# The start of the last feed-forward moved into the attention's last turn, with the last batch's end spread over its first steps

## What is computed

```python
q, k = heads(src @ Wq + bq), heads(src @ Wk + bk)          # 8 heads of 16
attn = softmax(q @ k.T / 4)                                # per batch 8 x 512 x 512
out = sum over r of (attn * (adj == r)) @ heads(src @ Wv[r] + bv[r])
x = layer_norm(src + out @ Wo + bo, g1, beta1)             # the attention's end
ff = gelu(x @ W1 + b1) @ W2 + b2                           # 128 -> 512 -> 128
return layer_norm(x + ff, g2, beta2)
```

## Time and profile before

| | us |
|---|---|
| median of 3 executions | 1179.6 (1178.28 to 1179.81) |
| the profiled execution, its own time | 1180.0 |
| its span, first to last instruction | 1178.2 |
| TensorE busy / VectorE / ScalarE / GpSimd | 1074.4 / 933.2 / 735.2 / 613.2 |
| granted TensorE clock, mean | 0.968 |
| last turn with a batch, its first to its last matmul | about 990 to 1021.7 |
| end of batch 15 alone | 1021.7 to 1038.3 |
| feed-forward | 1036.6 to the end |

### The profile page before, as it was taken

One profiled execution on the slowest core, in us unless ns is written; L12 is line 12 of the kernel. 1 busy time (PEld: TensorE's weight loads), 2 busy tenths in 40 slices (PEclk: granted clock), 3 DMA queues, 4 the chain that ended last, 5 costly groups with the idle time before them and its releaser, 6 DMA issues. The chain is left out here.

```text
span 1178.2 us, 21859 instructions
## 1 busy us (share of the span) xinstructions
PE 1074.4 (91%) x6087; PEld 515.6 (44%) x6087; DVE 933.2 (79%) x2324; ACT 735.2 (62%) x1341; POOL 613.2 (52%) x513
## 2 busy tenths in 40 slices
PE   3699999999988699999999999999999999889996
PEld 3666766767656223333333333333333333234442
DVE  2888888888897678888888889888888888337777
ACT  3477787777875366656666666666665665544442
POOL 3322322322212088888888888788878877700000
PEclk7699999999999799999999999999999999879998
DMA  5321131221104123322332233313331320000000
GB/s 164 112 108 54 53 106 54 66 94 53 53 32 140 36 85 109 98 65 82 112 94 77 66 112 94 87 56 115 101 93 39 116 64 2 1 5 31 36 36 36
DMA packets 49547, 86.54 MB, mean 73 GB/s; under 512 B 8920, under 2 KB 35928, under 8 KB 44379
## 3 DMA queue, kind: packets, MB, share of 16 engines
q1 hardware_dynamic: 46586, 85.59, 23.6%
q10 hardware_dynamic: 2912, 0.40, 0.2%
HBM read 52.12 MB, written 29.36 MB: 69 GB/s over the span
## 5 line engine op out<-in xcount | busy, mean ns | idle before, releaser
L1491 DVE TENSOR_REDUCE top<-b_peak 128x1 f32<-128x512 f32 x488 | 320.4, 685 | 75.4 <-PE b_peak L1243 73.9
L1365 ACT ACTIVATE b_prob<-b_score 128x1024 f32<-128x1024 f32 x256 | 257.9, 1026 | 157.1 <-PE b_score L1258 112.2
L1628 POOL TENSOR_TENSOR b_picked<-b_prob,mask 128x512 f32<-128x512 f32 x192 | 233.7, 1237 | 62.2 <-ACT b_prob L1365 48.6
L1628 POOL TENSOR_TENSOR b_picked<-b_prob,b_mask 128x512 f32<-128x512 f32 x192 | 235.5, 1249 | 48.7 <-ACT b_prob L1365 38.2
L467 POOL TENSOR_SCALAR a_code<-a_adj_in 128x512 bf16<-128x512 int32 x64 | 73.6, 1150 | 93.6 <-DVE a_xw_n L896 66.1
L1062 POOL TENSOR_TENSOR a_hw_n<-a_hw,a_inv 128x512 f32<-128x512 f32 x16 | 23.3, 1456 | 176.1 <-DVE a_inv L889 169.0
L833 ACT ACTIVATE a_att<-a_att,a_least 128x512 f32<-128x512 f32 x128 | 91.8, 720 | 31.3 <-DVE a_least L862 31.3
L1243 PE MATMUL b_peak<-b_k_stack,b_q_stack 96*128 96x512 bf16 x256 | 98.4, 384 | 7.1 <-DVE top L1491 6.5
L1243 PE MATMUL b_peak<-shared 96*128 96x512 bf16 x232 | 90.4, 391 | 10.0 <-issue 6.1
L862 DVE CUSTOM_DVE_ANT_0 a_att<-a_att,a_no_edge 128x512 f32<-128x512 f32 x128 | 89.5, 716 | 2.6 <-issue 2.1
L1745 ACT ACTIVATE c_hid<-c_mid,bff 128x512 f32<-128x512 f32 x64 | 44.0, 688 | 62.9 <-PE c_mid L1723 62.9
(11 more groups left out here) (216 smaller groups left out, 2018.4 us busy)
## 6 DMA issues: line engine op xcount, KB each, us to landing
a_adj_in<-in_adj SPq DMA_DIRECT2D x16, 1024.0 KB, 5.3
scratch<-shared SPq DMA_DIRECT2D x32, 384.0 KB, 2.9
shared<-scratch SPq DMA_DIRECT2D x16, 768.0 KB, 6.2
scratch<-shared SPq DMA_DIRECT2D x32, 256.0 KB, 2.1
b_q_stack<-scratch SPq DMA_DIRECT2D x8, 768.0 KB, 5.4
b_k_stack<-scratch SPq DMA_DIRECT2D x8, 768.0 KB, 8.2
a_x_in<-in_x SPq DMA_DIRECT2D x16, 256.0 KB, 2.6
xs<-in_x SPq DMA_DIRECT2D x16, 256.0 KB, 5.6
```

Of the source, the lines that this page charges most:

```text
L1365: act.activation(prob[s % 2][:, 2 * u:2 * u + 2, :], score[u][:, :, :], ACT.Exp, scale=float(DH) ** -0.5).then_inc(sem("exp_ready"), 1)
L1491: dve.tensor_reduce(top[g][:, hh, c:c + 1], peak[hh % 2][:, :], AX.X, ALU.max, negate=True).then_inc(sem("peak_read"), 1)
L1628: pool.tensor_tensor(picked[(NR * s + rel) % 2][:, hh, :], prob[s % 2][:, hh, :], m, ALU.mult).then_inc(sem("picked_pool"), 1)
```

## The change

The function `feed_forward` becomes a class `FeedForward` with the same operations as methods, called from the attention's streams. Its buffers now lie in the memory `shared` that held the stacks of the even batches, `hid` in the first q stack's place, the others in the first k stack's. Its banks are those of `score` and `peak`, with `o_ps` for `back`.

Turn 16 is gone. In its place every engine has a `last()`, and after it straight code in which the feed-forward's steps 0 to 3 and the end of batch 15 alternate. Feed-forward step 0 on TensorE stands before the last `weigh_picked`. The pieces `o1`, `turn_o`, `out` and `y` of batch 15 stand between the products of steps 1 and 2; its statistics, inverse root and shift on VectorE stand between `add` and `norm` of batch 2, and its centring on ScalarE before step 4. The inverse root of batch 15 is taken on VectorE with the 11 tiny instructions in place of Ln and Exp on ScalarE. Batches 4 to 15 run as before, in a loop.

In steps 1 to 7 of the turn of batch 15, GpSimd makes two of the four picked heads and VectorE two (`FREE = 1`).

```diff
+        FREE = 1
...
+        ff = FeedForward(z, w, xs, out, shared,
+                         (score[0][:, 0, :], [score[0][:, 1, :], score[1][:, 0, :], score[1][:, 1, :], peak[0][:, :]],
+                          peak[1][:, :], o_ps[:, :]), sem("centred"), sb, lambda name: keep.enter_context(nc.semaphore("c_" + name)))
...
-            for b in range(B - 2, B + 1):
+            for b in range(B - 2, B):
                 turn(b, b % 2)
+            last()
...
+        def pool_heads(b, s):
+            return POOL_HEADS - (isinstance(b, int) and b == B - 1 and s >= FREE)
+        def pool_picks(steps):
+            return POOL_HEADS * steps - (max(0, steps - S * (B - 1) - FREE) if isinstance(steps, int) else 0)
+        def vector_picks(steps):
+            return (GH - POOL_HEADS) * steps + (max(0, steps - S * (B - 1) - FREE) if isinstance(steps, int) else 0)
...
+            ff.store_all(sp)
...
-                turns(pe, turn)
+                def last():
+                    weigh_picked(B, 0, 0)
+                    weigh(B, 0, 0, None)
+                    pe.wait_ge(sem("peak_read"), S * B * GH)
+                    ff.turn_x(pe, 0)
+                    ff.up(pe, 0, 0)
+                    weigh_picked(B, 0, 1)
+                    pe.wait_ge(sem("misc_read"), reads_before(path, B, "o1"))
+                turns(pe, turn, last)
             both_paths(pe, run)
+            ff.turn_x(pe, 1)
+            ff.second(pe, 0)
+            pe.wait_ge(sem("o_t_ready"), G * B)
+            for c in range(C):
+                mm = pe.transpose(misc[:, c * P:(c + 1) * P], o_t[1][:, c * P:(c + 1) * P], ident[:, :])
+            mm.then_inc(sem("o1_done"), 1)
+            ff.up(pe, 1, 1)
+            pe.wait_ge(sem("last_read"), 1)
+            for c in range(C):
+                mm = pe.transpose(misc[:, c * P:(c + 1) * P], o[:, c, :], ident[:, :])
+            mm.then_inc(sem("turn_o_done"), 1)
+            ff.turn_back(pe, 0)
+            ff.turn_x(pe, 2)
+            ff.second(pe, 1)
+            pe.wait_ge(sem("last_read"), 2)
+            pe.matmul(misc[:, :], w["wo"][:, :], o_all_t[:, :], start=True, stop=True).then_inc(sem("out_done"), 1)
+            ff.up(pe, 2, 0)
+            pe.wait_ge(sem("last_read"), 3)
+            for c in range(C):
+                mm = pe.transpose(misc[:, c * P:(c + 1) * P], y_t[:, c * P:(c + 1) * P], ident[:, :])
+            mm.then_inc(sem("y_done"), 1)
+            ff.turn_back(pe, 1)
+            ff.tensor_step(pe, 3, 1)
+            with pe.Fori(2, B // 2) as half:
+                for k in range(2):
+                    ff.tensor_step(pe, 2 * half + k, k)
+            ff.second(pe, B - 1)
+            ff.turn_back(pe, B - 1)
...
-                            centre(b - 1, range(C) if isinstance(b, int) and b == B else (0, 1))
-                turns(act, turn)
+                            centre(b - 1, (0, 1))
+                def last():
+                    keep_o(B, 0, 0)
+                    centre(B - 2, (2, 3))
+                    ff.keep_x(act, 0, 0)
+                    ff.hidden(act, 0)
+                    keep_o(B, 0, 1)
+                turns(act, turn, last)
             both_paths(act, run)
+            for n in range(2):
+                act.wait_ge(sem(f"parts_out{n}"), 48 * B)
+            ff.keep_x(act, 1, 1)
+            ff.hidden(act, 1)
+            act.wait_ge(sem("centred"), C * (B - 1))
+            act.wait_ge(sem("turn_o_done"), B)
+            act.copy(o_all_t[:, :], misc[:, :]).then_inc(sem("last_read"), 1)
+            ff.keep_x(act, 2, 0)
+            ff.hidden(act, 2)
+            act.wait_ge(sem("y_done"), B)
+            act.copy(y[:, :, :], misc[:, :].rearrange("p (c d) -> p c d", c=C)).then_inc(sem("last_read"), 1)
+            ff.keep_x(act, 3, 1)
+            ff.hidden(act, 3)
+            act.wait_ge(sem("shift_ready"), B)
+            for c in range(C):
+                act.activation(xs[:, B - 1, c, :], y[:, c, :], ACT.Identity, bias=shift[:, c:c + 1],
+                               scale=rstd[:, c:c + 1]).then_inc(sem("centred"), 1)
+            with act.Fori(2, B // 2) as half:
+                for k in range(2):
+                    ff.keep_x(act, 2 * half + k, k)
+                    ff.hidden(act, 2 * half + k)
...
-                        for hh in range(POOL_HEADS, GH):
+                        for hh in range(pool_heads(b, s), GH):
...
-                turns(dve, turn)
+                def last():
+                    ff.take(dve, 0)
+                    pick(B, 0, 0)
+                turns(dve, turn, last)
             both_paths(dve, run)
+            ff.take(dve, 1)
+            ff.take(dve, 2)
+            ff.add(dve, 0, 0)
+            src = misc[:, :].rearrange("p (c h k) -> p c h k", c=C, h=GH)
+            dve.wait_ge(sem("turn_o_done"), B - 1)
+            dve.wait_ge(sem("o1_done"), B)
+            dve.reciprocal(inv[1][:, :, :], src[:, :, :, DH]).then_inc(sem("inv_ready1"), 1)
+            dve.wait_ge(sem("inv_ready1"), B)
+            dve.tensor_tensor(o[:, :, GH * DH:].rearrange("p c (h d) -> p c h d", h=GH), src[:, :, :, 0:DH],
+                              inv[1][:, :, :].unsqueeze(3).to_broadcast([P, C, GH, DH]), ALU.mult).then_inc(sem("last_read"), 1)
+            ff.norm(dve, 0)
+            ff.take(dve, 3)
+            ff.add(dve, 1, 1)
+            dve.wait_ge(sem("y_done"), B - 1)
+            dve.wait_ge(sem("out_done"), B)
+            dve.scalar_tensor_tensor(out=y_t[:, :], in0=misc[:, :], scalar=w["col"]["L1_gnn_bo"],
+                                     in1=xs[:, B - 1, :, :].rearrange("p c d -> p (c d)"),
+                                     op0=ALU.add, op1=ALU.add).then_inc(sem("last_read"), 1)
+            ff.norm(dve, 1)
+            ff.take(dve, 4)
+            ff.add(dve, 2, 0)
+            dve.wait_ge(sem("shift_ready"), B - 1)
+            dve.wait_ge(sem("last_read"), 4)
+            for c in range(C):
+                dve.bn_stats(stats[:, c, :], y[:, c, :]).then_inc(sem("stats_ready"), 1)
+            dve.wait_ge(sem("stats_ready"), C * B)
+            for c in range(C):
+                dve.bn_aggr(mv[:, c, :], stats[:, c, :]).then_inc(sem("mv_ready"), 1)
+            dve.wait_ge(sem("mv_ready"), C * B)
+            dve.wait_ge(sem("centred"), C * (B - 1))
+            ff.inverse_root(dve, ff.last_root, 0, mv, rstd)
+            dve.scalar_tensor_tensor(out=shift[:, :], in0=mv[:, :, 0], scalar=-1.0, in1=rstd[:, :],
+                                     op0=ALU.mult, op1=ALU.mult).then_inc(sem("shift_ready"), 1)
+            ff.norm(dve, 2)
+            ff.take(dve, 5)
+            ff.add(dve, 3, 1)
+            ff.norm(dve, 3)
+            with dve.Fori(2, B // 2 - 1) as half:
+                for k in range(2):
+                    t = 2 * half + k + 1
+                    ff.take(dve, t + 1)
+                    ff.add(dve, t - 1, k)
+                    ff.norm(dve, t - 1)
+            for b in range(B - 2, B):
+                ff.add(dve, b, b % 2)
+                ff.norm(dve, b)
...
-                        for hh in range(POOL_HEADS):
+                        for hh in range(pool_heads(b, s)):
...
+    def __init__(self, z, w, xs, out, shared, banks, attended, sb, sem):
+        self.z, self.w, self.xs, self.out, self.attended = z, w, xs, out, attended
+        N, C, D, FC = z.N, z.C, z.D, z.FC
+        at = [0]
+        def take(words):
+            at[0] += words
+            return shared[:, at[0] - words:at[0]]
+        def rows(flat):
+            return flat.rearrange("p (c d) -> p c d", c=C)
+        self.hid = take(FC * N).rearrange("p (f n) -> p f n", f=FC)
+        self.y_t, self.y, self.res, x_t0 = take(N), rows(take(C * D)), rows(take(C * D)), take(N)
+        self.x_own = rows(take(C * D))
+        take(N)
+        self.x_t = [x_t0, take(N)]
+        self.stats, self.mv = sb("c_stats", [P, C, 6]), sb("c_mv", [P, C, 2])
+        self.var, self.square, self.rstd = sb("c_var", [P, C]), sb("c_square", [P, C]), sb("c_rstd", [P, C])
+        self.turn, self.mid, self.down, self.back = banks
...
+    def tensor_step(self, pe, t, par):
+        self.turn_x(pe, t)
+        self.second(pe, t - 1)
+        self.up(pe, t, par)
+        self.turn_back(pe, t - 1)
...
+    def take(self, dve, t):
+        dve.wait_ge(self.turned, t)
+        dve.wait_ge(self.attended, self.z.C * (t + 1))
+        dve.tensor_copy(self.x_own[:, :, :], self.xs[:, t, :, :]).then_inc(self.own, 1)
+    def add(self, dve, b, par):
+        dve.wait_ge(self.x_t_ready, b + 1)
+        dve.wait_ge(self.backed, b)
+        dve.wait_ge(self.down_done, b + 1)
+        dve.scalar_tensor_tensor(out=self.y_t[:, :], in0=self.down, scalar=self.w["col"]["L1_gnn_b2"], in1=self.x_t[par][:, :],
+                                 op0=ALU.add, op1=ALU.add).then_inc(self.summed, 1)
...
```

(20 more changed lines are left out.)

244 lines of the change are left out of this document (92 added, 152 removed).

## The result

The changed kernel takes 1168.0 us (median of 4, 1167.32 to 1170.93) against 1179.4: a ratio of 0.990, 95% interval 0.988 to 0.992, so about 1% faster and clear of no change. The forecast was 1165.3, in a range of 1163.2 to 1169.7. The profiled execution has 1167.3 us and a span of 1165.5.

A forecast was written before the change was run, and what follows sets the result against it. TensorE's start of the feed-forward, behind a serial chain of about 15 us, was the bound. The stretch falls from 54.8 to 41.8 us; 13.0 + 1.3 = 14.3 off 1180.0 gives 1165.7, against the median 1165.3; range 1163.2 to 1169.7.

The forecast's parts named there:

- The bound and the stretch: From the last probability weighing to the end of `c_back` of batch 3, 54.8 us before; only this stretch should change.
- Part 1: Batch 15's steps 1 to 7: GpSimd gives up a head per step, gaining 1.3 us, bounds 0 and 2.0.
- if the steps of the last turn stay at 3.6 us: Sign that the prediction is wrong, read on the steps of batch 15's turn.
- The price of 0.4 us: Batch 15's steps under the skill's shared-port rule: 3.67 us a step, the sum about 0.4 us later.
- Part 2: Feed-forward start: first product begins 1.5 us after the last probability weighing; table load and leaving the If cost nothing.
- Part 3: TensorE's queue from the first product to the end of `c_down` of batch 3: 33.8 us, batch 15's pieces adding 2.2.
- The tightest reply: VectorE's sum for `y` of batch 15 comes at +20.7, TensorE gets there at +21.2, 0.5 us to spare.
- Part 4: Batch 15's norm in step 4: late replies make TensorE wait 1.7 and 0.9 us; `c_back` of batch 3 ends at +40.3.
- The clock: TensorE's granted clock: no fall taken, the bound being one fall worth 3.4 us.
- The rival of a fall in step 4: TensorE's clock falls after step 4's waits of 1.7 and 0.9 us: 1168.7 us, chance 0.16.
- The lost balance: Rival: each of the twelve steady feed-forward steps behind waits 0.2 us, giving 1167.7 us, chance 0.08.
- Port contention: Rival, batch 15's steps 1 to 7: picks at their longest, seven steps lose 21 us, 1188 us, chance 0.02.

The follow-up runs named there:

- changed_beside: The changed kernel again without an edit, timed beside other edited versions: 1166.6 us, ratio 0.9878 to the kernel before.
- mask_from_psum: Changed kernel, VectorE's picks in batch 15's steps 2 to 6 multiplying by PSUM contents, not the SBUF mask; ran once, first `c_mid` 1.7 us sooner than with the change.
- root_twice: Changed kernel with batch 15's inverse root computed twice on VectorE, 11 tiny instructions more: 1171.5 us, ratio 0.9928 to the kernel before.
- root_shared: Changed kernel with batch 15's inverse root in batch 2's instructions and its centring behind batch 4's Gelus: 1168.1 us, ratio 0.9910 to the kernel before.
- centre_later: Changed kernel with ScalarE's centring of batch 15 moved behind the Gelus of batch 4: 1170.0 us, ratio 0.9919 to the kernel before.
- mixed_heads: Changed kernel with GpSimd giving up a head only in batch 15's steps 2, 4 and 5; ran once, first `c_mid` 1.1 us sooner.

## Why the prediction was right, and where it wasn't

**The bound and the stretch** were read rightly. Behind `c_back` of batch 3 nothing changed: 102.26 us to the end before, 102.25 after (102.61 in `changed_beside`, with the slower last transposes). All of the gain lies where the prediction looked.

**Part 1, the head moved off GpSimd, was wrong in sign.** The failed step is "it becomes the bound and the gain is what it waits now: 1.43 us", taken as 1.3. Measured is a loss of 0.7, 2.0 us away and outside the stated bounds (0 to 2.0 gained). The sum counted VectorE's extra time as lying beside TensorE because VectorE was idle for half of that turn, and priced the engines' collisions by what GpSimd lost per pick (0.36 us). What decides is what VectorE loses where its picks bunch. In step 6 its two picks take 3.17 us in a row beside GpSimd's, and TensorE waits 1.14 us for the second; step 3 adds a wait of 0.41. The row for it was there, VectorE's maximum of 1.64 us in the earlier trace rows, and the prediction used it only as a bound. `mask_from_psum` turned the +0.7 into -1.0 with the same number of picks on each engine. The prediction had named the sign of this: it is wrong "if the steps of the last turn stay at 3.6 us", and they did (21.8 us for six).

The prediction set a rule of the Trainium skill against this part ("SBUF — State Buffer", section "Who interferes with whom"). The mechanism is the one that these runs show: the long picks go when one of VectorE's two inputs lies in PSUM. The price of 0.4 us that the prediction drew from it does not follow from its own numbers, since 3.67 less 3.3 us is 0.4 for one step and not for the turn. At 3.67 us a step, an estimate from that rule and the durations of the earlier trace rows, six steps take 22.0 us; measured are 21.8, and 21.2 before. So the rule, worked through, had the sign. That its size fits too is partly luck: GpSimd was busy for only 15.64 of 23.10 us, and the loss comes in two steps.

**Part 2, the start,** holds: from the end of the last probability weighing (1021.99) to the first product 1.5 us, as forecast; the first Gelu at +1.3 and the fourth's end at +4.4, under cover of `c_mid` and the last weighing. TensorE leaves the If with no hole that the records show.

**Part 3, the queue,** holds: TensorE is ready for `c_mid` of batch 4 at 34.1 us after the first product, forecast 33.8. The tightest reply, VectorE's sum for `y`, ends at +21.0 and TensorE gets there at +21.5 (20.7 and 21.2), with the 0.5 us to spare that the prediction gave.

**Part 4, the late norm,** holds in each term. VectorE's and ScalarE's timelines:

```profile
1052.76 0.86 DVE L1721 BATCH_NORM_STATS2 b_stats<-b_y 128x6 f32<-128x128 f32 x4
...
1056.24 0.16 DVE L1728 SCALAR_TENSOR_TENSOR b_shift<-b_mv,b_rstd 128x4 f32<-128x4 f32 x1
1056.32 0.88 DVE L1921 BATCH_NORM_STATS2 b_c_stats<-b_o_ps 128x6 f32<-128x128 f32 x4
```

```profile
1056.44 1.65 ACT L1557 ACTIVATE xs<-b_y,b_shift,b_rstd 128x128 f32<-128x128 f32 x4 [2.40 <-DVE b_shift L1728]
1057.99 0.76 ACT L1876 ACTIVATE shared<-b_score,columns 128x512 f32<-128x512 f32 x1
```

The shift ends at +32.9 (forecast 32.8), the scale at +35.2 (35.4), `c_back` of batch 3 at +40.4 (40.3). The two waits are 1.18 and 0.75 us where 1.7 and 0.9 were forecast, because TensorE is 0.3 us later itself and the two replies come 0.1 to 0.2 us sooner. `root_twice` and `root_shared` confirm from both sides that VectorE's queue sets this, and `centre_later` that ScalarE's wait is not a second price on top of it.

**The clock** stayed at 1.00, as taken. The rival of a fall in step 4 did not come in any of the three profiles of the changed kernel, but it is near: a wait of 3.37 us at that place brought one in `root_twice`. **The lost balance** did not come either; the lateness of step 4 is paid once. **Port contention** as a rival had the right mechanism and far too high a price: 0.66 us against before, not 21.

**The number.** With part 1 as measured the prediction's sum gives 1165.7 + 2.0 = 1167.7 us for the profiled execution. It took 1167.3, and the 0.4 between is the arrival at A, 998.24 us in place of 998.64. Against the median the same sum gives 1167.3; the first four executions have 1168.0. That a forecast with part 1 wrong in sign still has the time in its range is luck in part: the range ran up to 1169.7 to allow for a fall of the clock and a lost balance, and neither came. The part's error took up that room. The three comparisons put the gain at 9.7 to 14.4 us (0.9918 and 0.9878 of about 1180), so the median's own agreement says less than the stretches do.

## What to carry to other kernels

Before work moves to an engine that looks half idle, ask whether it touches the same operands at the same moment as the engine it is taken from: the longest duration of such an instruction, not its median or the engine's busy share, is its price in the step where two of them come together (1.67 us against 0.68 here). A chain that made TensorE wait at two places, for two engines, had one price here and not two; double one part of it, and take the other away, to see which engine holds it. Tiny dependent instructions cost their count and hardly their width (0.17 us on eight columns, 0.16 on four), so a second small root can ride in the first one's instructions.

## What the runs showed of the hardware that was not expected

- A VectorE product with both operands in SBUF takes 0.68 us, but up to 1.67 us while GpSimd multiplies from SBUF, and GpSimd's goes from 1.16 to 1.61. With one operand in PSUM ten of ten took 0.65 to 0.69 us.
- The copy of a batch, 128x512 in SBUF, took 0.42 us alone, 0.76 us beside GpSimd's picks in the changed kernel and 1.22 in `mixed_heads`.
- TensorE's clock fell behind a wait of 3.37 us in the feed-forward (`root_twice`), and stayed at 1.00 behind waits of 1.18 and 0.75 us and, in `centre_later`, of 2.22. In the kernel before it fell behind the shorter wait of 1.95 us. Before the last transposes the same wait of 3.22 us in the same kernel ended at the full clock in one execution and at the half clock in another. So in these traces the length of one wait does not tell whether the clock falls.
